# Graph layer with additive attention: the projection made one batch ahead, half of the attention weights beside units 4 to 7

## What is computed

```python
h = jnp.maximum(_layernorm(x, axis=-1), 0.0)          # per channel, over the nodes
q = jnp.einsum('c,bcn->bn', wq, h)
k = jnp.einsum('c,bcn->bn', wk, h)
scores = q[:, None, :] + k[:, :, None]
scores = jnp.where(scores > 0, scores, 0.01 * scores)
att = jax.nn.softmax(scores, axis=-1)
agg = jnp.einsum('bcn,bmn->bcm', h, att)
out = relu(jnp.einsum('oc,bcm->bom', adj, agg) + bm[None, :, None])
return x + out
```

## Time and profile before

| | |
|---|---|
| median of 3 runs | 2118.74 us (2117.84 to 2120.95) |
| the profiled execution | 2118.1 us |
| its span, first to last instruction | 2116.4 us |
| TensorE busy | 2055.2 us, 97% |
| VectorE busy | 1635.0 us, 77% |
| ScalarE busy | 1219.7 us, 58% |
| GpSimd busy | 389.6 us, 18% |
| DMA engines busy (mean of 16) | 49.7% |
| read and written | 202.91 and 67.63 MB |

### The profile page before, as it was taken

One profiled execution on the slowest core, in us unless ns is written; L12 is line 12 of the kernel. 1 busy time (PEld: TensorE's weight loads), 2 busy tenths in 40 slices (PEclk: granted clock), 3 DMA queues, 4 the chain that ended last, 5 costly groups with the idle time before them and its releaser, 6 DMA issues.

```text
span 2116.4 us, 33329 instructions
## 1 busy us (share of the span) xinstructions
PE 2055.2 (97%) x10416; PEld 946.0 (45%) x10416; DVE 1635.0 (77%) x3633; ACT 1219.7 (58%) x1873; POOL 389.6 (18%) x266
## 2 busy tenths in 40 slices
PE   5599999999999999999999999999999999999999
PEld 2244444444444444444444444444444444444444
DVE  6877788778888777787778787788787777877753
ACT  3565555655646665556655556555566655566543
POOL 0012211112212112111122211122111122111221
PEclk9799999999999999999999999999999999999999
DMA  4255544555544565444555444555445654445441
GB/s 169 95 145 140 131 115 130 135 148 139 126 96 152 130 154 139 97 122 140 139 149 135 109 123 136 144 139 131 96 147 130 154 139 104 117 144 138 114 100 40
DMA packets 178622, 271.48 MB, mean 128 GB/s; under 512 B 87648, under 2 KB 87648, under 8 KB 170336
## 3 DMA queue, kind: packets, MB, share of 16 engines
q1 hardware_dynamic: 178528, 270.59, 49.7%
HBM read 202.91 MB, written 67.63 MB: 128 GB/s over the span
## 4 chain that ended last, share of the span: by engine, by line
PE 80%; DVE 10%; issue 7%; DMA 1%; ACT 1%; SPq 0%; DVEq 0%; POOLq 0%
PE mix L352 15%; PE mix L353 15%; PE mix L354 15%; PE mix L333 11%; PE mix L335 10%; PE mix L334 10%; DVE den_out L639 4%; DVE p_ring L659 4%; DVE p_lo L666 2%; PE small L307 1%; PE small L316 1%; DMA ab_rows<-ab_col 1%; DMA wm_nat<-in_adj_dram 0%; ACT v_hi L444 0%; DVE v_lo L671 0%
## 5 line engine op out<-in xcount | busy, mean ns | idle before, releaser
L352 PE MATMUL mix<-p_hi,v_hi 128*128 128x512 f16 x2048 | 777.3, 380 | 8.3 <-DVE p_lo L666 8.3
L354 PE MATMUL mix<-p_hi,v_lo 128*128 128x512 f16 x2048 | 777.0, 379 | 0.0
L353 PE MATMUL mix<-p_lo,v_hi 128*128 128x512 f16 x2048 | 777.0, 379 | 0.0
L768 POOL TENSOR_TENSOR res<-res,y 128x512 f32<-128x512 f32 x256 | 386.1, 1508 | 1706.7 <-ACT y L451 1706.7
L432 ACT ACTIVATE p_ring<-ab_row,cols 128x512 f32<-128x512 f32 x512 | 349.4, 692 | 168.3 <-DVE p_lo L666 155.1
L659 DVE SCALAR_TENSOR_TENSOR p_ring<-ab_row,cols,p_ring 128x512 f32<-128x512 f32 x512 | 376.7, 747 | 61.9 <-ACT p_ring L432 32.7
L333 PE MATMUL mix<-wmT_hi,h_hi 128*128 128x512 f16 x1024 | 389.4, 380 | 0.0
L335 PE MATMUL mix<-wmT_hi,h_lo 128*128 128x512 f16 x1024 | 389.1, 380 | 0.0
L334 PE MATMUL mix<-wmT_lo,h_hi 128*128 128x512 f16 x1024 | 389.1, 380 | 0.0
L639 DVE SCALAR_TENSOR_TENSOR den_out<-den_row,cols 128x512 f32<-128x512 f32 x512 | 371.8, 763 | 0.0
L666 DVE SCALAR_TENSOR_TENSOR p_lo<-p_ring,p_hi 128x512 f16<-128x512 f32 x512 | 349.4, 682 | 5.3 <-ACT p_hi L440 5.1
(11 more groups left out here) (60 smaller groups left out, 692.6 us busy)
## 6 DMA issues: line engine op xcount, KB each, us to landing
xs<-in_x_dram SPq DMA_DIRECT2D x128, 512.0 KB, 6.1
res<-in_x_dram SPq DMA_DIRECT2D x256, 256.0 KB, 3.5
out_dram<-res SPq DMA_DIRECT2D x256, 256.0 KB, 2.4
den_row<-den_rows SPq DMA_DIRECT2D x32, 1024.0 KB, 4.7
ab_row<-ab_rows SPq DMA_DIRECT2D x32, 1024.0 KB, 6.2
wm_nat<-in_adj_dram SPq DMA_DIRECT2D x1, 1024.0 KB, 9.4
den_rows<-cols SPq DMA_DIRECT2D x32, 8.0 KB, 1.6
ab_rows<-ab_col SPq DMA_DIRECT2D x32, 8.0 KB
```

Source lines behind the costliest of these rows:

```text
L352: pe.matmul(ps[:, :], v_hi[:, nt, chans], p_hi[:, hf, nt, :], start=(nt == 0), stop=False)
L353: pe.matmul(ps[:, :], v_hi[:, nt, chans], p_lo[:, hf, nt, :], start=False, stop=False)
L354: mm = pe.matmul(ps[:, :], v_lo[:, nt, chans], p_hi[:, hf, nt, :], start=False, stop=(nt == NT - 1))
L768: pool.tensor_tensor(res[:, k, :], res[:, k, :], y[:, k % 2, :], ALU.add).then_inc(s_add, 1)
```

## The change

- **Projection one batch ahead.** v_hi and v_lo get room for two batches. TensorE's period is now the eight units of b and then `v_phase(b+2)`: project_qk and the eight projection tiles of b+2, with select_qk behind tile 1 and spread_qmax behind tile 3. Before the first period both the first and the second batch are projected. The last two periods have no projection.
- **Half of the weights beside units 4 to 7.** Half 0 of the weights of b+1 is made in the period of b before the projection, not beside it; the projection's v_upper and v_lower stand alone, with the q steps.
- **Normalisation.** The activations of `normalise` (now `h_upper` and `h_full`) stand between the steps of half 1 on ScalarE; `statistics` and `normaliser` of b+3 stand beside the projection of b+2 on VectorE, the normaliser between v_lower of tiles 6 and 7. x of b+3 is loaded ahead of store 5 instead of behind store 6.
- **Row scales.** VectorE writes them into a 128 by 128 tile (ab_pad); `transpose_ab`, a TensorE transposition inside unit 4 ahead of node tile 4, waits for them, `copy_ab` (VectorE) copies 16 by 128 numbers, and the write to DRAM has 512 contiguous bytes in each row. The load back is in two halves with a semaphore for each.
- **Start.** The weights are loaded from ScalarE's queue, x of the second batch into the residual tile; the first batch's h_full of two tiles is made by VectorE.
- VectorE's loop has 13 rounds instead of 14.

The diff, cut to the steady periods and what they call:

```diff
@@ sync @@
             def write_ab_rows(b):
-                sp.wait_ge(s_dn, cnt(b, D_OPS, D_OPS))
-                with nc.allow_non_contiguous_dma(reason="2048 floats into node order"):
-                    sp.dma_start(ab_dram.rearrange("r t p -> p r t"), ab_col[:, :, :]).then_inc(s_aw, 16)
+                sp.wait_ge(s_at, cnt(b, 1, 1))
+                sp.dma_start(ab_dram.rearrange("r t p -> (r t) p"), ab_t[:, :]).then_inc(s_aw, 16)
...
                 for k in range(1, U):
+                    if one and k == 4:
+                        write_ab_rows(nxt(b))
+                        load_ab_rows(nxt(b))
                     store(b, k)
                     if one:
                         load_residual(nxt(b), k - 1)
-                        if k == 3:
-                            write_ab_rows(nxt(b))
-                        if k == 4:
-                            load_ab_rows(nxt(b))
-                    if three and k == 6:
+                    if three and k == 4:
                         for c in range(CT):
                             load_x(nxt(b, 3), c)
@@ tensor @@
+            def transpose_ab(b):
+                if at(b, first):
+                    pe.wait_ge(s_az, 1)
+                    pe.wait_ge(s_qc, Q_OPS + 4)
+                pe.wait_ge(s_dn, cnt(b, D_OPS, D_OPS))
+                pe.transpose(ab_ps, ab_pad[:, :], ident[:, :]).then_inc(s_aT, 1)
...
                 for nt in range(NT):
-                    if k == 0:
-                        pe.wait_ge(s_vlo[nt % 2], cnt(b, NT // 2, nt // 2 + 1))
+                    if one and k == MIX and nt == 4:
+                        transpose_ab(nxt(b))
+                    if k == 0 and nt < 2:
+                        pe.wait_ge(s_vlo[nt], cnt(b, NT // 2, NT // 2))
...
+            def v_phase(b):
+                project_qk(b)
+                for nt in range(NT):
+                    if nt == 2:
+                        select_qk(b)
+                    if nt == 4:
+                        spread_qmax(b)
+                    v_tile(b, nt)
+
             def period(b, one, two):
                 for k in range(U):
-                    unit(b, k)
-                if one:
-                    for nt in range(NT):
-                        if two and nt == 2:
-                            project_qk(nxt(b, 2))
-                        if two and nt == 3:
-                            select_qk(nxt(b, 2))
-                        if two and nt == 5:
-                            spread_qmax(nxt(b, 2))
-                        v_tile(nxt(b), nt)
+                    unit(b, k, one)
+                if two:
+                    v_phase(nxt(b, 2))
@@ scalar @@
                 for nt in range(NT):
                     p_upper(b, NT + nt)
                     if nt < NT - 2:
                         leak(b, NT + nt + 2)
...
+                    if two and nt in (0, 3, 7):
+                        h_upper(h, (0, 3, 7).index(nt))
+                    if two and nt in (1, 5):
+                        h_full(h, nt // 4)
+                    if nt in (2, 4, 6):
+                        relu(b, nt // 2 - 1)
+                if two:
+                    h_upper(h, 3)
                 relu(b, 3)
+                if two:
+                    h_full(h, 2)
+                    h_full(h, 3)
                 relu(b, 4)
+                if one:
+                    n = nxt(b)
+                    leak(n, 0)
+                    leak(n, 1)
+                    for nt in range(NT):
+                        p_upper(n, nt)
+                        if nt < NT - 2:
+                            leak(n, nt + 2)
+                        if nt == 0:
+                            relu(b, 5)
+                        if nt == 4:
+                            relu(b, 6)
...
+                relu(b, 7)
                 if two:
-                    normalise(nxt(b, 2), 3)
-                relu(b, 7)
-                if one:
-                    v_slots(nxt(b), two)
+                    for nt in range(NT):
+                        v_upper(h, nt)
+                        if nt == 4:
+                            exponentials(h)
@@ vector @@
+            def copy_ab(b):
+                dve.wait_ge(s_aT, cnt(b, 1, 1))
+                dve.tensor_copy(ab_t[:, :], ab_ps[0:2 * NT, :]).then_inc(s_at, 1)
...
+            def half_0(b):
                 weight(b, 0)
                 for nt in range(NT):
                     if nt < NT - 1:
                         weight(b, nt + 1)
-                    v_lower(b, nt)
                     p_lower(b, nt)
...
                 if one:
                     row_scales(nxt(b))
                 if two:
-                    for ct in range(CT):
-                        statistics(nxt(b, 2), ct)
-                    normaliser(nxt(b, 2))
-                    for ct in range(CT):
-                        h_lower(nxt(b, 2), ct)
+                    h_lower(h, 0)
+                    h_lower(h, 1)
                 if one:
-                    v_slots(nxt(b), two)
+                    copy_ab(nxt(b))
+                if two:
+                    h_lower(h, 2)
+                    h_lower(h, 3)
+                if one:
+                    half_0(nxt(b))
+                if two:
+                    q_rows(h)
+                    for nt in range(NT):
+                        v_lower(h, nt)
+                        if nt == 1:
+                            q_head(h)
+                        if nt == 3:
+                            q_tail(h)
+                        if three and 2 <= nt < 2 + CT:
+                            statistics(nxt(b, 3), nt - 2)
+                        if three and nt == 6:
+                            normaliser(nxt(b, 3))
```

The start, on TensorE and VectorE:

```diff
             project_qk(second)
-            select_qk(second)
-            spread_qmax(second)
+            for nt in range(NT):
+                if nt == 1:
+                    select_qk(second)
+                if nt == 2:
+                    spread_qmax(second)
+                if nt == 4:
+                    transpose_ab(first)
+                v_tile(second, nt)
@@ vector @@
+            q_rows(first)
             weights_lower()
-            q_rows(first)
             q_head(first)
             q_tail(first)
+            for ct in range(CT):
+                statistics(second, ct)
             v_lower(first, 0)
...
+            normaliser(second)
             v_lower(first, 1)
...
+            denominator(first, 0)
+            v_lower(first, 2)
+            denominator(first, 1)
             for ct in range(CT):
                 h_lower(second, ct)
+                v_lower(first, 3 + ct)
+                denominator(first, 2 + ct)
+            v_lower(first, 7)
+            q_rows(second)
+            denominator(first, 6)
+            q_head(second)
+            denominator(first, 7)
+            row_scales(first)
```

255 lines of the change are left out of this document (144 added, 111 removed).

## The result

The changed kernel takes **2245.14 us** (median of 4 runs, 2242.45 to 2246.45) against 2119.12 (2117.84 to 2120.95) for the kernel before: ratio 1.0595, interval 1.0582 to 1.0608, slower by 126 us. I had predicted 2156, within 2135 to 2175. The side was right, the size was not.

The account below looks back on a forecast made before the run. TensorE was taken as the limit. 2116.4 + 0.9 (start) - 22.3 (one projection) - 10.7 (old holes) = 2084.3, plus 69.1 of waits at transpositions: span 2153.4, time 2156 us, range 2135 to 2175 (chance 0.70).

Parts of the forecast that it names:

- What bounds it, and where it would wait: TensorE is the limit and waits in unit 4 for the row scales in every period, 2.2 us in the mean.
- The half: VectorE's second half of the weights begins at T+2.5 in plain periods, T being the start of unit 0.
- p_lo wait: TensorE's wait for the last p_lo of unit 4 at every second batch goes: 10.7 us less.
- 12 stops: One at each jump of VectorE's loop, with a transposition wait of 3.75 us each: 45.0 us in all.
- the hole at the start: TensorE's nearly idle stretch from 58 to 81 is filled with projection matmuls; units start near 81 to 82.
- 22.3 us that the sum takes off: One of 31 projections is done before the first unit: 22.28 us less behind the start.
- The stop at the jump: VectorE stops 2.32 us at its loop's jump, so the half starts at T+4.8; price 3.75 us, bounds 2.9 to 4.5.
- The clock: Rival: TensorE's clock falls after stops of 3.75 us, 1.9 us lost at each, 25 us in all: 2181; chance 0.10.
- The chain from the half to the row scales: On VectorE it keeps its 21.87 us, so the row scales end at T+24.37 in plain periods.
- The plain price: TensorE's wait at the transposition without a jump: 1.23 us, bounds 0.7 to 1.8; 20.9 us in 17 periods.
- the first transposition's wait: In the first period, row scales at 111.6 where TensorE would be at 108.7: 3 us.
- the row scales arrive sooner: Rival: no jump stop and a shorter normaliser; all 31 waits 0.3 to 0.8 us, time 2095 to 2112; chance 0.13.

Follow-up runs that it names:

- the run with the filling: Changed kernel with 24 matmuls of unused result on TensorE directly ahead of the transposition: 2271.42 us, ratio 1.0718 to the kernel before.
- the two padded kernels: Changed kernel with 107 or 214 further instructions that do nothing ahead of VectorE's loop: 2224.86 and 2259.26 us, a single run each.
- the kernels without a stop: Changed kernel with VectorE's loop written out, 2157.0 us, and changed kernel with 8 further do-nothing instructions ahead of the loop, 2159.32 us.

## Why the prediction was right and wrong

**What bounds it, and where it would wait: right.** TensorE reaches the transposition before the row scales in every period. The half begins at T+2.40 (forecast T+2.5) by the normaliser ahead of v_lo of tile 7; moving the normaliser moved it by as much. No p_lo wait to speak of, 12 stops, the hole at the start filled with a projection (T = 81.56 against "near 81 to 82"): all as put. Only the size of that gain was 1.6 us too high: of the 22.3 us that the sum takes off, 20.7 are the projection, and the rest the q and k matmuls, which were not moved.

**The stop at the jump: wrong size, the largest term.** "The stop was 2.32 us behind the last operation. I add it to T+2.5" took the length of the stop from the earlier trace rows as a property of the jump. It is one of the body's place: 4.8 here, 2.4 with 107 or 214 instructions more ahead of it, none with 8. What TensorE loses at the wait behind a jump is 7.17 us in the mean (a step of 7.12, less the usual 0.216, plus 0.26 for the transposition) instead of 3.75: 2.5 more from this, 0.9 from the chain.

**The clock: given as a rival at 0.10, and it came.** It fell at every jump (12 steps of 6.85 to 7.36 us), which I priced at 1.9 us for a stop of 3.75; measured some 2.3 by the run with the filling, and 2.2 as what the periods leave (73.12 - 67.47 - 3.4). The experiments also show that I weighed it wrongly at my own size: behind the steps of 4.7 to 5.1 us in the two padded kernels it fell every time, and also behind the pair of 2.6 to 3.0 and 1.5 us with the transposition in unit 5.

**The chain from the half to the row scales: 1.0 too short.** "With the same 21.87 us" assumed that a chain of the same operations moved by 0.4 us has the same length. Its bounds covered the first addition (0.15 or 0.62), but that one was already at 0.62 in the window of the earlier trace rows:

```profile
1069.29 0.62 DVE L646 TENSOR_TENSOR den<-den_part 128x8 f32<-128x8 f32 x1
```

What changed was a den_out that begins just behind GpSimd's addition (0.07 in the tail shown) and takes 1.75 us. That it comes wherever the half begins speaks for the new order and not for the 0.4 us; what in the order brings the two together was not separated. The plain price became 2.2 us instead of 1.23, outside my bound of 1.8.

The sum, in spans: forecast 2153.4, measured 2244.7, 91.3 more. Periods behind a jump 12 × 5.65 = 67.8 (12 × 3.4 = 41 by the longer hole, 12 × 2.2 = 27 by the clock); plain periods 17 × 1.06 = 18.0; the start and the first period 3.8 (the second period begins at 156.84, forecast 153.0; 1.2 of it by the first transposition's wait, 4.2 us instead of 3.0, and 1.7 by eight slow steps behind it); the end 1.7, nearly all of it the 1.6 us that the projection was priced too high. The rival "the row scales arrive sooner" put the stop's disappearance at 2126 with the normaliser as forecast; the kernels without a stop gave 2157 and 2159, since the chain was longer too. That its condition can be met by eight idle instructions was not in the profile of before.

## What to carry to other kernels

A wait put on the bounding engine must be priced with the worst arrival of every period, and where its two sides are within a microsecond, a slot a few microseconds later can cost nothing: here 5.2 us later turned 31 waits at the transposition into none. The unexplained "issue" stop at the loop's jump went here with the place of the code; an edit of the engine's list that has nothing to do with it can double or remove such a stop. So cut the loop where the engine idles anyway, and judge an edit with the loop written out before it is blamed or praised.

## What the runs showed of the hardware that I had not expected

- The stop at a loop's jump on VectorE was 0, 2.4 or 4.8 us for the same body of some 340 instructions, by the number of instructions ahead of it (8, 107 or 214, none). It consists of a pause of 2.8 to 3.1 us at the jump and, where the body begins at 397 or 399, a second of 2.1 to 2.5 us at place 401.
- A VectorE operation with two inputs in SBUF that began 0.07 us behind a GpSimd addition took 1.75 instead of 0.74 us, and an addition of 128x8 took 0.61 instead of 0.17. One that began 0.15 us ahead of GpSimd's took 0.74.
- A write of the same 8 KB took 11.8 us as single numbers from 128 partitions and 1.4 as 16 contiguous rows.
- TensorE's clock fell to 1.2 GHz behind every step of 4.3 us and more in which it started nothing, and gave 5 to 13 steps of 0.427 us each time in the kernels with the wait at the transposition. Of the 13 plain steps of 2.48 to 2.51 us in the kernel with 214 instructions more it followed ten; of those of 2.2 to 2.3 in the plain periods of the kernel after, one of 17 (the step of 2.28 at 180); and in the kernel with the loop written out, with steps of 2.21 to 2.27, none behind the first period.
